# Scatter the codes of two tiles in three from GpSimd, and divide the work of the edge row passes otherwise, in a fused graph-network kernel

## The reference, cut to what matters

```python
x = layernorm(x + L0(x, edge_attr, dst))       # segment sum of 160 attributes, 2 products, softplus
x = layernorm(x + L1(x, edge_weight, src, dst))# weighted mean of neighbours, 2 products
x = layernorm(x + L2(x, src, dst))             # relu(x @ w_s + sum of neighbours @ w_n)
x = layernorm(x + L3(x, src, dst))             # two Chebyshev convolutions of order 3
# in L3: deg = count of edges per src (src != dst), dis = deg ** -0.5 where deg > 0
#        w   = -dis[src] * dis[dst]
```

## Time and profile before

| | |
|---|---|
| median of 3 runs | 4458.62 us (4454.08 to 4461.81) |
| the profiled execution | 4466.06 us, of which the span from first to last instruction is 4464.0 us |
| PE, DVE, ACT, POOL busy | 80%, 71%, 55%, 67% of the span |
| mean granted clock of PE | 0.889 |
| the count | from 23.7 to about 291 us |
| tgt0 | from 311 to about 668 us |
| src0 | from 669 to about 1180 us |
| nodes, then the six edge passes | to 2577 us, then to the end |

### The profile page before, as it was taken

The page is one execution under the profiler, slowest core; times in us unless marked ns, Lnnn a source line. Parts: engine busy times, 40 slices in busy tenths (PEclk is TensorE's granted clock), DMA queues, the critical chain, the costliest instruction groups (busy, mean ns, idle before and its releaser), DMA issues. The chain is left out here.

```text
span 4464.0 us, 77093 instructions
## 1 busy us (share of the span) xinstructions
PE 3560.5 (80%) x21778; PEld 2728.0 (61%) x21778; DVE 3173.4 (71%) x13414; ACT 2444.6 (55%) x7163; POOL 3007.1 (67%) x3450
## 2 busy tenths in 40 slices
PE   6868887999899999999999956566898989931111
PEld 3336655766588888888888746565455768831111
DVE  8988876677588888888888868788222446655555
ACT  0006665666588888888888856311565764421111
POOL 0006656555388888888888767576775757767777
PEclk9989997888899999999999978888999999965555
DMA  0015643444222222222222235454676987843332
GB/s 19 1 45 155 166 133 127 164 166 167 100 77 77 77 76 77 76 76 76 77 77 77 68 123 156 127 157 143 221 247 217 310 288 247 260 140 93 98 94 77
DMA packets 307439, 575.11 MB, mean 129 GB/s; under 512 B 65310, under 2 KB 93783, under 8 KB 307018
## 3 DMA queue, kind: packets, MB, share of 16 engines
q1 hardware_dynamic: 234890, 442.75, 29.4%
q0 software_dynamic: 72128, 127.43, 10.9%
HBM read 300.83 MB, written 270.68 MB: 128 GB/s over the span
## 5 line engine op out<-in xcount | busy, mean ns | idle before, releaser
L1316 PE MATMUL ps<-ident,rows 128*128 128x128 f32 x1372 | 280.9, 310 | 605.2 <-ACT rows L1093 498.3
L540 POOL DMA_INDIRECT rows<-state,rows_of_src x588 | 557.4, 948 | 252.6 <-issue 171.7
L1093 ACT ACTIVATE rows<-rows,lap_w 128x128 f32<-128x128 f32 (+1 forms) x784 | 270.7, 419 | 607.3 <-DMA rows<-lap,rows_of_lap 480.0
L1316 PEld LDWEIGHTS ps<-ident,rows 128*128 128x128 f32 x1372 | 191.4, 159 | 672.7 <-ACT rows L1093 453.6
L810 DVE TENSOR_TENSOR_SCAN x<-same,x,ps 128x512 f32<-128x512 uint8 x336 | 429.0, 1277 | 236.5 <-PE ps L1316 204.6
L1076 ACT ACTIVATE yTa<-ps 128x512 f32<-128x512 f32 x392 | 233.5, 596 | 607.8 <-PE ps L1298 607.6
L540 POOL DMA_INDIRECT rows<-lap,rows_of_lap x392 | 390.5, 996 | 168.5 <-issue 117.1
L618 POOL DMA_INDIRECT lk<-node_table,look_idx x392 | 384.6, 981 | 92.1 <-issue 83.6
L575 POOL TENSOR_TENSOR y<-xin,c0h 128x512 f32<-128x512 f32 x245 | 310.8, 1269 | 200.0 <-DVE outb L982 142.6
L926 DVE BATCH_NORM_STATS2 bn<-y 128x6 f32<-128x128 f32 x1764 | 378.6, 276 | 42.8 <-POOL y L575 42.7
L1454 PE MATMUL ps<-V,hT 128*128 128x128 f32 x3136 | 402.0, 281 | 5.5 <-ACT hT L1206 5.5
(11 more groups left out here) (253 smaller groups left out, 9601.1 us busy)
## 6 DMA issues: line engine op xcount, KB each, us to landing
state_h<-hb SPq DMA_DIRECT2D x98, 512.0 KB, 3.9
xin<-in_x_dram SPq DMA_DIRECT2D x196, 256.0 KB, 2.8
out_dram<-outb SPq DMA_DIRECT2D x196, 256.0 KB, 2.1
xe<-state SPq DMA_DIRECT2D x147, 256.0 KB
state<-outb SPq DMA_DIRECT2D x98, 256.0 KB, 2.1
state<-oe SPq DMA_DIRECT2D x98, 256.0 KB, 2.1
h_pre<-hb SPq DMA_DIRECT2D x49, 512.0 KB, 3.1
rows<-in_edge_attr_10x_dram SPq DMA_DIRECT2D x48, 320.0 KB, 3.2
```

Source lines behind the costliest of these rows:

```text
L540: gp.indirect_dma_start(out=dest[:, at, k, 0:width], out_offset=None, in_=table_, in_offset=bass.IndirectOffsetOnAxis(ap=index[:, c:c + 1] ...
L1316: i = t.transpose(bank(g.b)[:, k, :], rows[:, g.r, k, 0:P], ident[:, :])
```

## The change

1. The count: tiles with c % 3 == 0 (66, `COUNTED`) are counted as before. For the other 130 (`PUT`) DVE makes only `bin_s` and `lane_s`, PE multiplies only the source count, and POOL scatters each edge's code, four bytes per edge, into `node_put` in DRAM (rows of edges that are not the last of their destination lie out of bounds and are dropped). SP writes zeros there first, and reads it back into `put_back` when all 130 have landed; DVE adds it to the codes.
2. tgt0: `put_weights` stands ahead of the gathers in POOL's turn and is for turn g+3; the weights' column is turned by four transposes in place of four products.
3. src0: the fourth `x3b` slice is scaled by POOL, behind its gathers and after rs1; h's bias is added by DVE at the end of its turn, 128x1024 into `hb`, and no longer by PE; ACT's Relu works in place on `hb` at the end of its turn; the store of `x3b` waits for both writers.

```diff
+            sp.dma_start(node_put.rearrange("(p n) c -> p (n c)", p=P), put_back).then_inc(put_zeroed, 16)
 ...
+            sp.wait_ge(code_put, 16 * len(PUT))
+            sp.dma_start(put_back, node_put.rearrange("(p n) c -> p (n c)", p=P)).then_inc(codes_in, 16)
             sp.wait_ge(vstep, V_TABLE)
...
+            gp.memset(put_back, 0.0)
...
+            pool.wait_ge(put_zeroed, 16)
+            pool.wait_ge(vstep, V_COLS)
+            for c in PUT:
+                gp.indirect_dma_start(out=node_put, in_=put_code[:, c:c + 1], in_offset=None, bounds_check=P * BINS - 1,
+                                      oob_is_err=False,
+                                      out_offset=bass.IndirectOffsetOnAxis(ap=put_row[:, c:c + 1], axis=0))\
+                    .then_inc(code_put, 16)
...
+                put_weights(g.less(-3))
                 gather("tgt0", g, x, dst_g, xin, g.b, P, x_gathered, [(step, 2)])
-                put_weights(g.less(-2))
...
+                    if p == "src0" and g1.inside(n):
+                        rs1.wait(pool, p, g1)
+                        more_st.wait(pool, p, g1, back=2)
+                        gp.tensor_scalar(x3b[:, g1.b, 3, :], y1[:, g1.b, 3, :], rs[:, 1, g1.b, 3:4], None, ALU.mult)\
+                            .then_inc(x2_made.sem, 1)
...
+            v.scalar_tensor_tensor(put_code, v_tile, float(P), v_lane, ALU.mult, ALU.add)
+            link(v.tensor_copy(look_f, look_idx[:, :, 1]))
+            v.tensor_tensor(put_row, t_f, look_f, ALU.add)
...
                 v.tensor_scalar(bin_s, iota_bin, a_src[:, c], None, ALU.is_equal)
-                v.tensor_scalar(bin_d, iota_bin, a_dst[:, c], None, ALU.is_equal)
-                v.tensor_scalar(lane_s, iota_lane, b_src[:, c], mask[:, c], ALU.is_equal, ALU.mult)
-                v.tensor_scalar(lane_t, iota_lane, b_dst[:, c], v_tile[:, c], ALU.is_equal, ALU.mult)
-                v.tensor_scalar(lane_l, iota_lane, b_dst[:, c], v_lane[:, c], ALU.is_equal, ALU.mult)\
-                    .then_inc(hots, 1)
+                i = v.tensor_scalar(lane_s, iota_lane, b_src[:, c], mask[:, c], ALU.is_equal, ALU.mult)
+                if g.c in COUNTED:
+                    v.tensor_scalar(bin_d, iota_bin, a_dst[:, c], None, ALU.is_equal)
+                    v.tensor_scalar(lane_t, iota_lane, b_dst[:, c], v_tile[:, c], ALU.is_equal, ALU.mult)
+                    i = v.tensor_scalar(lane_l, iota_lane, b_dst[:, c], v_lane[:, c], ALU.is_equal, ALU.mult)
+                i.then_inc(hots, 1)
...
+            dve.wait_ge(codes_in, 16)
+            v.tensor_tensor(table[:, :, 0], table[:, :, 0], put_back, ALU.add)
...
-                            for k in range(4):
+                            for k in range(3):
                                 i = v.tensor_scalar(x3b[:, g1.b, k, :], y1[:, g1.b, k, :], dev(1, g1.b, k), None, ALU.mult)
-                            i.then_inc(x2_made.sem, 1)
+                            i.then_inc(x2_most.sem, 1)
+                    if i3 and not nodes:
+                        h_made.wait(dve, p, g3)
+                        h_st.wait(dve, p, g3, back=2)
+                        v.tensor_tensor(hb[:, g3.b], wide(5), all4(gb1_row[:, :]), ALU.add).then_inc(h_biased.sem, 1)
...
-                    if g4.inside(n) and not nodes:
-                        h_made.wait(act, p, g4)
-                        h_st.wait(act, p, g4, back=2)
-                        a.activation(hb[:, g4.b], wide(5), ACT.Relu).then_inc(h_kept.sem, 1)
...
+                    if g4.inside(n) and not nodes:
+                        h_biased.wait(act, p, g4)
+                        a.activation(hb[:, g4.b], hb[:, g4.b], ACT.Relu).then_inc(h_kept.sem, 1)
...
+                    if bk and g.c not in COUNTED:
+                        continue
...
-                            i = t.matmul(ps[:, 4, k:k + 1], agg_b[32:33, g.b, k, :], ones[32:33, 0:1], start=True, stop=True)
+                            i = t.transpose(ps[:, 4, k:k + 1], agg_b[32:33, g.b, k, :], ident[32:33, 32:33])
...
-                            h_kept.wait(pe, p, g3, back=1)
+                            h_biased.wait(pe, p, g3, back=1)
                             for k in range(4):
-                                t.matmul(wide(5)[:, k, :], ones[0:1, :], gb1_row[0:1, :], start=True, stop=False)
-                                i = t.matmul(wide(5)[:, k, :], yTc[:, k, :], G02[:, :], start=False, stop=True)
+                                i = t.matmul(wide(5)[:, k, :], yTc[:, k, :], G02[:, :], start=True, stop=True)
```

More of the change, by code:

```diff
@@ L128, in gnn_kernel @@
         node_table = dram("node_table", (P * BINS, 2))
+        node_put = dram("node_put", (P * BINS, 1))
         def one(v, g):
@@ L241, in gnn_kernel @@
             signal(n, "nodes") for n in ("y3_made", "bn3", "mv3", "rs3", "off3_made", "looked_up"))
-        x1_made, rs1, x2_made, off2 = (signal(n, "src0") for n in ("x1_made", "rs1", "x2_made", "off2"))
+        x1_made, rs1, x2_made, x2_most, h_biased, off2 = (
+            signal(n, "src0") for n in ("x1_made", "rs1", "x2_made", "x2_most", "h_biased", "off2"))
         same_made, ew_put, ws_turned, ws_taken, ws_max = (
@@ L279, in gnn_kernel @@
                              "alink", "dlink", "roots_in", "hots", "counted"))
-        edges_in, as_float, listed, lanes_made = (sem(n) for n in ("edges_in", "as_float", "listed", "lanes_made"))
+        edges_in, as_float, listed, put_zeroed, code_put, codes_in = (
+            sem(n) for n in ("edges_in", "as_float", "listed", "put_zeroed", "code_put", "codes_in"))
         seam, padded = sem("seam"), sem("padded")
@@ L305, in gnn_kernel @@
         s2_i, t_f, has = cols(outb, 0, I32), cols(outb, 1), cols(outb, 2)
+        put_row, put_code, look_f = cols(outb, 3, I32), cols(outb, 4), cols(y1, 4)
+        put_back = hT[:].rearrange("p a k d -> p (a k d)")[:, 0:BINS]
         hot = hb[:].rearrange("p a k d -> p (a k d)").bitcast(F16)
@@ L321, in gnn_kernel @@
         LOADS, EDGE_LOADS = 15, 12
+        COUNTED = [c for c in range(TILES) if c % 3 == 0]
+        PUT = [c for c in range(TILES) if c % 3 != 0]
         V_COLS, V_WEIGHTS, V_BTC, V_TABLE = 1, 2, 3, 4
@@ L471, in src0_turn @@
                         signal_.wait(sp, "src0", g_)
+                        if signal_ is x2_made:
+                            x2_most.wait(sp, "src0", g_)
                         sp.dma_start(quad_of(t, g_, 1), buf[:, g_.b]).then_inc(tr.of(g_), 16)
@@ L558, in tgt0_turn @@
                     gp.memset(rows[:, last.r, 3, 0:ATTR], 0.0).then_inc(zeroed, 1)
+                put_weights(g.less(-3))
                 gather("tgt0", g, x, dst_g, xin, g.b, P, x_gathered, [(step, 2)])
-                put_weights(g.less(-2))
-            put_weights(Turn(0))
-            put_weights(Turn(1))
+            for c in range(3):
+                put_weights(Turn(c))
             run_turns(QUADS, 0, tgt0_turn)
@@ L578, in turn @@
                 def turn(g):
-                    next_, g2, g3 = g.less(-1), g.less(2), g.less(3)
+                    next_, g1, g2, g3 = g.less(-1), g.less(1), g.less(2), g.less(3)
                     if next_.inside(n):
@@ L974, in turn @@
                         squared.wait(dve, p, g, back=2)
+                        if not nodes:
+                            x2_made.wait(dve, p, g, back=2)
                         for k in range(4):
@@ L1269, in count_tile @@
             def count_tile(g):
-                first, last = (g.c == c for c in (0, TILES - 1))
                 pe.wait_ge(hots, g.lin(1, 1))
@@ L1273, in count_tile @@
                 for bk, lanes, bins in ((0, lane_s, bin_s), (2, lane_t, bin_d), (4, lane_l, bin_d)):
+                    if bk and g.c not in COUNTED:
+                        continue
+                    first, last = (g.c == c for c in ((COUNTED[0], COUNTED[-1]) if bk else (0, TILES - 1)))
                     for j, (lo, n) in enumerate(((0, 512), (512, BINS - 512))):
```

## The result

| | before | after |
|---|---|---|
| median of the runs (us) | 4457.76 (4454.08 to 4461.81, 4 runs) | 4291.93 (4290.96 to 4299.25, 4 runs) |
| profiled execution, span (us) | 4464.0 | 4289.2 |
| mean granted clock | 0.889 | 0.902 |

The ratio is 0.9631 [0.9615, 0.9648]: 166 us gained where 65 were forecast. Cutting both traces at the same events gives the stages. The first row ends where SP begins to store the table; tgt0 with the last start of 880 (913 after), src0 with the last start of the reciprocal rs1 (1018, 1053 after), its tail with the first lookup of the node pass, nodes with the last one.

The account below looks back on a forecast made before the run. It took DVE to bound the count, a loop through four engines tgt0, and PE src0. Count -45, tgt0 -36, src0 +15 and tail +1 sum to -65: 4458.6 - 65 = 4394 us, range 4305 to 4450.

Parts of the forecast that it names:

- The count: Count: three tiles (one counted, two scattered) take 3.35 us, scatters hidden behind them; 45 us gained.
- third rival: Count: DVE starves POOL's scatters, so the codes come 186 us late; 4580 us in all; chance 0.09.
- second rival: Count: PE drops to its lower clock, 1.2 GHz; half of it gives 4425 us; chance 0.14.
- tgt0: Pass tgt0: PE's transposes no longer wait for POOL, turn falls from 6.74 to 6.0 us; 36 us gained.
- So DVE's second slice waits until y0 is done: In src0: POOL's slice and the y0 behind it hold up DVE's second x3b slice; 1.67 us more a turn.
- the collision: In src0: POOL's slice and y0 meeting DVE's slices, lengthening the turn from 8.1 to about 9.75 us; 15 us lost.
- the first rival: In src0: POOL's slice and y0 don't catch DVE, turn 8.1 to 8.6 us; 4327 us in all; chance 0.27.
- The tail: End of src0: grows by 1 us for the bias moved to DVE.
- The sum: Whole kernel: -45 - 36 + 15 + 1 = -65 us, from 4458.6 to 4394 us.

Follow-up runs that it names:

- slice_tt: The changed kernel with POOL's x3b slice in src0 as a product of two tensors instead of a scaling by a column; 4350.29 us, ratio 0.9751.
- y0_first: The changed kernel with POOL starting y0 upon rs1 and doing its x3b slice behind it; 4339.56 us, ratio 0.9729.
- bias_on_pe_c: The changed kernel with src0's bias back on PE as one-row matmuls and Relu reading from the bank; 4367.51 us, ratio 0.9806.

## Why the prediction was wrong, point by point

- **The count: right.** -47.3 where -45 was forecast; 3.33 us for a triple and 3.35 forecast, made as worked out: DVE waits 0.71 us in each for PE's six matmuls (forecast 0.78). The scatters took 0.99 us each and hid. The third rival (scatters starved) did not come, and DVE waited for no code. The second rival (PE's lower clock) did not come either: 1.00 in the count.
- **tgt0: right in mechanism, 9 us short.** The turn is 5.91 us against 6.0; POOL's column no longer stands before PE's transposes. The other 5.4 us lie ahead of the first 880 (30.9 us from the table before, 25.5 after), a stretch for which I had no term.
- **src0: the step that failed.** "So DVE's second slice waits until y0 is done", 1.67 us a turn. It does not wait. What failed is the form: my rows showed only POOL instructions with two inputs (575, 585), and I carried them over to a slice with one. Beside that one DVE's slices go on, at a median of 0.32 us (the second 0.39) instead of 0.28. The time was off too: I let y0 begin 0.59 us after the burst's start (0.16 + 0.43), and it came at 0.73, since POOL's slice took 0.69 us where the same form takes 0.44 in the node pass (line 619). But DVE's last slice had begun at 0.51, ahead of either. slice_tt and y0_first bring y0 ahead of the second slice, and with it 1.07 and 0.91 us of the 1.67. My turn without the collision, 8.1 us, was met (8.07), in part by luck: the burst alone took 0.84 us and not 0.88 less 0.20, and something that no run names gave the 0.16 back. That was the first rival, which I gave 0.27.
- **The tail: missed.** Forecast +1, measured -13.5. I had priced PE's lost pairs at their full rate. In the last two turns PE has gaps ahead of them, and the timeline of before has G and bias at half rate, eight pairs in 9.3 us; after, G alone takes 2 to 2.9 us. bias_on_pe_c brings the 12 us back.

The timeline of before in that tail, and the one of after for the same work:

```profile
1163.28 1.22 PE L1466 MATMUL ps<-gb_row,ones 1*128 1x256 f32 x2 [0.75 <-ACT yTc L1076]
1164.43 1.22 PE L1467 MATMUL ps<-G,yTc 128*128 128x256 f32 x2
...
1171.33 1.22 PE L1467 MATMUL ps<-G,yTc 128*128 128x256 f32 x2
```

```profile
996.81 2.88 PE L1506 MATMUL ps<-G,yTc 128*128 128x256 f32 x8 [1.85 <-DVE hb L1062]
```

- **What the one-row matmuls were worth.** I read the 0.86 of src0 and took it as given, and priced four pairs at 2.5 us a turn, with 6.9 left for PE. PE was busy 232.69 / 340 x 8.07 = 5.5 us: the clock came back, and G alone takes 1.99 us where G and bias took 4.9 at full rate. Both belonged to the very instructions that the change removes. This did not spoil the turn, because DVE took over as the limit at 8.07; it does say that moving the bias to DVE was not needed. With 128 rows PE keeps it, and the turn is 7.1 us.
- **The sum.** From the rival's 4327 us, src0's 65 for 52 takes 13, the tail 14.5, tgt0 9, the count 2 and the rest 3: 4284. The other 8 to the 4292 measured are the profiled executions, which lie otherwise to their medians than I took. The range ended at 4305: the first rival's best end with every other term at its middle is 4315, so that 10 us were left for the tail, tgt0 and the count, which all came out better together, and by more.

## What to carry to other kernels

A meeting of two engines in a trace prices only the form of instruction and the moment that it shows: before carrying it over, compare the number of inputs in SBUF on both sides, and work out which instruction begins first. Where PE is full and one-row matmuls alternate with 128-row ones, compare the distance of the pairs and the granted clock, and try to give them 128 rows before moving them elsewhere. Time a kernel whose GpSimd scatters run beside a dense stage on more than one chip.

## What was not expected of the hardware

- One-row matmuls alternating with 128-row ones: pairs 0.63 us apart at full clock, and 0.43 when all have 128 rows; PE 99% busy at 0.86 with them, 96% busy at 1.00 without; 9.42 and 7.12 us a turn.
- POOL's tensor_scalar in f32 beside DVE's: 0.69 us where it took 0.44 in the node pass, and 0.32 in place of 0.28 for DVE's, no shutting out. POOL's tensor_tensor in its place: 0.53 us for DVE's slice beside it, and up to 1.71 us for the one beside the y0 that follows. The Trainium skill ("SBUF — State Buffer", section "Who interferes with whom") says that whichever of the two issues first holds the shared ports for its whole instruction; y0 in slice_tt agrees with that, since it began 0.05 us ahead of DVE's second slice, which ended behind it; in the changed kernel the slices of both engines ran side by side, and neither waited for the whole of the other.
- 130 scatters of 0.99 us ran beside f16 scaling that filled 77% of DVE's time, and were not starved. On two chips of five the opposite came: the scatters kept their pace and the count's tiles went from 1.10 to 1.86 us.
